# A fourth pair of weight chunks by seven products in the last two blocks, and mixed weights made by GpSimd in the first and second

## The reference

```python
xn = layernorm(x)
s = silu(xn @ w_gate.T)                       # 2752 gate units
_, idx = top_k(-abs(s), 1376)                 # the smaller half of each token's gates by magnitude ...
s = s.at[rows, idx].set(0.0)                  # ... is set to 0
a = (s * (xn @ w_up.T)) @ w_down.T
h = relu(xn @ up_w) ** 2                      # 2048 shared units
moe = ((xn @ fc1_w) @ expert_w) * sum(top_k(xn @ gate_w, 2)[0])
f = layernorm(h @ down_w + moe @ fc2_w, gamma, beta)
y = x + a + f
```

## The kernel before

| m | step |
|---|---|
| 0-7 | the last, narrow gate chunk (5), with the router's logits |
| 8-91 | three pairs of chunks by seven products each, 28 granules a pair: gate 0 and 1, gate 2 and 3, gate 4 and up 4 |
| 92-123 | latent, hidden 0 and 1, routed 0 and 1 |
| 124-171 | shared 0 and 1, hidden 2 and 3, shared 2 and 3 |
| 172-203 | up chunks 0 to 3, 8 granules each |
| 204-247 | out 0 and 1, 22 granules each |

## Time and profile before

### The profile page before, as it was taken

How to read it: one execution, slowest core, us unless ns; L and a number is a source line. 1 busy time by engine, 2 the same in 40 slices (tenths; PEclk the granted TensorE clock), 3 DMA queues, 4 the chain that set the end, 5 groups by cost and what they waited for, 6 DMA issues and landing times.

```text
span 2333.7 us, 27748 instructions
## 1 busy us (share of the span) xinstructions
PE 2317.7 (99%) x10504; PEld 1927.2 (83%) x10504; DVE 1634.8 (70%) x1810; ACT 1086.9 (47%) x1253; POOL 829.3 (36%) x682
## 2 busy tenths in 40 slices
PE   8999999999999999999999999999999999999999
PEld 6888888888877888888888888888888888888887
DVE  4349999976265989897334598898723568989850
ACT  3247776223233787722124387761213448785110
POOL 5467878796444021123024321304004413030500
PEclk9999999999999999999999999999999999999999
DMA  7798878878898666665778766665667865556555
GB/s 277 280 394 294 292 245 311 293 243 310 287 363 302 206 196 191 204 201 180 234 237 277 249 194 193 195 209 189 207 219 255 279 221 195 193 192 214 180 190 180
DMA packets 191047, 558.43 MB, mean 239 GB/s; under 512 B 20161, under 2 KB 29377, under 8 KB 190913
## 3 DMA queue, kind: packets, MB, share of 16 engines
q1 hardware_dynamic: 190912, 556.65, 71.0%
HBM read 429.62 MB, written 126.94 MB: 238 GB/s over the span
## 4 chain that ended last, share of the span: by engine, by line
PE 93%; DMA 3%; DVE 1%; SPq 1%; POOL 1%; ACT 0%; issue 0%; DVEq 0%; ACTq 0%
PE bank L945 30%; PE bank L947 30%; PE bank L946 30%; PE bank L965 2%; DMA mixed_w<-mixes 1%; DMA split_w<-w 1%; DMA w<-mixed_w 1%; PE bank L956 1%; POOL w L732 0%; SPq L565 0%; SPq L569 0%; PE bank L1038 0%; PE bank L1039 0%; DMA raw<-w_gate_dram 0%; POOL w L735 0%
## 5 line engine op out<-in xcount | busy, mean ns | idle before, releaser
L1292 DVE TENSOR_SCALAR_CACHE_REDUCE junk_v<-mag,cand 128x2816 bf16<-128x2816 f32 x248 | 780.3, 3146 | 8.8
L786 ACT ACTIVATE junk_s<-mag,cand 128x2816 uint8<-128x2816 f32 x248 | 655.4, 2643 | 222.2 <-DVE cand L1284 195.7
L945 PE MATMUL bank<-w,tok 128*128 128x512 f32 (+1 forms) x952 | 365.8, 384 | 1.8 <-DMA w<-split_w 1.7
L947 PE MATMUL bank<-w,tok 128*128 128x512 f32 (+1 forms) x952 | 364.3, 383 | 0.0
L946 PE MATMUL bank<-w,tok 128*128 128x512 f32 (+1 forms) x952 | 364.1, 382 | 0.0
L732 POOL TENSOR_TENSOR w<-raw,w 128x512 fp32r<-128x512 f32 (+1 forms) x196 | 268.1, 1372 | 77.5 <-ACT w L774 67.8
L945 PE MATMUL bank<-w,prod_t 128*128 128x512 f32 x672 | 269.4, 401 | 0.0
L947 PE MATMUL bank<-w,prod_t 128*128 128x512 f32 x672 | 262.8, 391 | 0.0
L946 PE MATMUL bank<-w,prod_t 128*128 128x512 f32 x672 | 261.9, 390 | 0.0
L945 PE MATMUL bank<-tok,w 128*128 128x512 f32 x640 | 249.0, 389 | 0.0
L946 PE MATMUL bank<-tok,w 128*128 128x512 f32 x640 | 249.0, 389 | 0.0
(11 more groups left out here) (149 smaller groups left out, 3728.3 us busy)
## 6 DMA issues: line engine op xcount, KB each, us to landing
...
split_w<-w SPq DMA_DIRECT2D x192, 512.0 KB, 4.9
...
w<-mixed_w SPq DMA_DIRECT2D x108, 256.0 KB, 3.5
...
```

What stands on the lines that cost most here:

```text
L786: act.activation(junk_s[:, :, :], mag[:, :, t, :], ACT.Sign, scale=-1.0, bias=cand[:, t:t + 1], accum_out=cnt[:, t:t + 1]).then_inc(counte ...
L945: pe.matmul(out, left[0], right[0], start=first, stop=False)
L947: return pe.matmul(out, left[1], right[0], start=False, stop=last)
L1292: dve.tensor_scalar(junk_v[:, :, :], mag[:, :, t, :], cand[:, t:t + 1], float(1 - (GATED - KEPT)), ALU.is_lt, ALU.add, accum_out=cnt[:, t: ...
```

## The change

In blocks 2 and 3 a fourth pair, up chunks 0 and 1, is made by seven products behind the third, and the plain steps of these two chunks are left out (`FAST`). These blocks have 260 granules: pairs 8 to 119, latent from 120, shared 2 and 3 to 199, up 2 and 3 from 200 to 215, `out` from 216. The first turn stands behind granule 211, and bank 0 holds up chunk 2 there as before.

- `prod` can't hold `S3` and `S4` and the results of this pair, so in blocks 2 and 3 these sums lie in `acc` and are split at granules 10 and 12, once the last block's outputs are stored (`sums_acc`).
- The hidden units need the rows of up 0 and 1, so SP writes these results, 1 MB a chunk, to DRAM behind the pair (`spill`, at granule 123) and loads them back behind shared 3 (`load_back`, at 199). VectorE gives each its sign (`sign_up`, now with `g`) right ahead of its mask.
- Two steps of the search stand beside the fourth pair (granules 101 and 108), the other 29 at 122 to 199, every 2.75 granules; `drop_ties` at 202, masks from 203 on. Shared chunk 3 is read at 203.
- The third pair's mixes are made in block 0 and the fourth's in block 1, one set of four operations per k-step, by GpSimd (`late_mix`) at `at + 11`, in `raw_more` or `raw`. SP loads a set's four pieces at `at` to `at + 6` and stores four at `at + 14`, with `at` = 36, 54, 72, 90 in block 0 and 96, 114, 132, 150 in block 1. `mix_later` and what belonged to it are gone.

```diff
...
-PAIRS = [(("gate", 0), ("gate", 1)), (("gate", 2), ("gate", 3)), (("gate", GC - 2), ("up", GC - 2))]
-FAST = len(PAIRS)
+PAIRS = [(("gate", 0), ("gate", 1)), (("gate", 2), ("gate", 3)), (("gate", GC - 2), ("up", GC - 2)),
+         (("up", 0), ("up", 1))]
+FAST = [0, 3, 4, 4]
 FIRST_PAIRS = 2
+UP_PAIR, SPILLED_PAIR = 2, 3
 PRODUCTS = ["A11 B11", "S2 T2", "A12 B21", "S1 T1", "S4 B22", "S3 T3", "A22 T4"]
-PRODUCT_BANK = [[4, 6, 0, 2, 4, 6, 0], [2, 4, 6, 4, 6, 0, 2], [4, 6, 0, 4, 6, 0, 2]]
+PRODUCT_BANK = [[4, 6, 0, 2, 4, 6, 0], [2, 4, 6, 4, 6, 0, 2], [4, 6, 0, 4, 6, 0, 2],
+                [4, 6, 0, 4, 6, 0, 2]]
...
-        steps = _middle + _last
+        steps = [step for step in _middle + _last if step[0] not in sum(PAIRS[:FAST[b]], ())]
...
+            self.signs_at = {end["fast", p, q] + FAST_LAG + 3: (p, q) for p in range(UP_PAIR) for q in (5, 6)}
+            up_end = end["fast", UP_PAIR, 6]
+            self.signs_at[last + 4 if up_end == last else up_end + FAST_LAG + 3] = (UP_PAIR, 6)
+        if later and FAST[b] > SPILLED_PAIR:
+            first = up_end + FAST_LAG + 4
+            steps_at = [first, first + 7]
+            steps_at += [last + 3 + (11 * k + 3) // 4 for k in range(BITS + 1 - len(steps_at))]
         else:
-            self.search_from = end[("gate", GC - 2)] + LAG + 1
-        self.search_at = {self.search_from + 3 * k: k for k in range(BITS)}
-        self.search_end = self.search_from + 3 * BITS
+            first = last + 5 if later else end[("gate", GC - 2)] + LAG + 1
+            steps_at = [first + 3 * k for k in range(BITS + 1)]
+        self.search_at = {m: k for k, m in enumerate(steps_at[:BITS])}
+        self.search_from, self.search_end = first, steps_at[BITS]
...
-        self.mask_at = {max(self.search_end + 1 + i, end.get(("up", g), 0) + LAG + 1): g
+        self.back_at = end[("shared", 3)] if FAST[b] > SPILLED_PAIR else None
+        read = {("up", c): self.back_at + 5 + 2 * c for c in range(2)} if self.back_at else {}
+        read.update({key: end[key] + LAG for key in end})
+        self.mask_at = {max(self.search_end + 1 + i, read.get(("up", g), 0) + 1): g
                         for i, g in enumerate(GROUPS[:-1])}
...
-MIX_BLOCK = 1
-MIX_LOADS = {8: range(8, 10), 32: range(10, 11), 40: range(11, 12)}
-MIX_AT = {24: 8, 32: 9, 44: 10, 52: 11}
-MIX_STORES = {26: 8, 34: 9, 46: 10, 54: 11}
+LATE_SETS = {FIRST_MIXES + n: (0, 36 + 18 * n) for n in range(HALF)}
+LATE_SETS.update({FIRST_MIXES + HALF + n: (1, 96 + 18 * n) for n in range(HALF)})
+LATE_LOADS = [{at + 2 * i: (n, i) for n, (b, at) in LATE_SETS.items() for i in range(4) if b == c} for c in range(BLOCKS)]
+LATE_AT = [{at + 11: n for n, (b, at) in LATE_SETS.items() if b == c} for c in range(BLOCKS)]
+LATE_STORES = [{at + 14: n for n, (b, at) in LATE_SETS.items() if b == c} for c in range(BLOCKS)]
...
-SUMS_HI_AT = {2: 4, 4: 3}
-SUMS_LO_AT = {2: 4, 4: 3}
+SUMS_HI_AT = [{}, {2: 4, 4: 3}, {10: 4, 12: 3}, {10: 4, 12: 3}]
+SUMS_LO_AT = [{}, {2: 4, 4: 3}, {10: 4, 12: 3}, {10: 4, 12: 3}]
...
+        sums_acc = {i: [over(f"sums{i}_acc{part}", [P, HALF, 2 * P], F32R, acc_at + 8 * N * (2 * (i - 3) + part))
+                        for part in range(2)] for i in (3, 4)}
+        assert 32 * N == TILES * HID * 4
+        def sums_of(b, i):
+            return sums_acc[i] if i > 2 and FAST[b] > SPILLED_PAIR else sums[i]
...
-            def load_mix(n):
+            def load_late_mix(n, i):
                 p, k = n // HALF, n % HALF
-                if n < FIRST_MIXES + 2:
-                    sp.wait_ge(stored, 16 * (MIX_BLOCK * 2 * TILES + 1))
+                if n == FIRST_MIXES:
+                    sp.wait_ge(mixes_made, 4 * FIRST_MIXES)
                 else:
-                    sp.wait_ge(mixes_stored[n % 2], 16 * (n // 2))
-                for i in range(4):
-                    src, width = words_of((PAIRS[p][i // 2], k + i % 2 * HALF))
-                    sp.dma_start(mix_place(n, i), src).then_inc(mix_loaded[n % 2], 16)
-            def store_later_mix(n):
-                sp.wait_ge(later_mixes, 4 * (n - FIRST_MIXES) + 4)
-                words = acc[:, 2 * (n % 2):2 * (n % 2) + 2, :].rearrange("p t (i n) -> p t i n", n=N)
-                sp.dma_start(mixed_w[n].rearrange("(t i) p n -> p t i n", i=2), words).then_inc(mixes_stored[n % 2], 16)
+                    sp.wait_ge(late_stored, 64 * (n - FIRST_MIXES))
+                if n in LATE_AT[1].values():
+                    sp.wait_ge(lo_ready, FIRST_PLAN.count)
+                src, width = words_of((PAIRS[p][i // 2], k + i % 2 * HALF))
+                sp.dma_start(late_place(n, i), src).then_inc(late_loaded, 16)
+            def store_late_mix(n, i):
+                sp.wait_ge(late_mixes, 4 * (n - FIRST_MIXES) + 4)
+                sp.dma_start(mixed_w[n, i], late_place(n, i)).then_inc(late_stored, 16)
+            def spill(b, c):
+                for q in (4, 5) if c else (2, 6):
+                    for j in range(2):
+                        bank, value = emptied(b, ("fast", SPILLED_PAIR, q, j))
+                        sp.wait_ge(bank_emptied[bank], value)
+                sp.dma_start(spilled_u[c], prod[:, 4 * c:4 * c + 4, :, :]).then_inc(spilled[c], 16)
+            def load_back(b, c):
+                sp.wait_ge(spilled[c], 16 * spills(b))
+                sp.dma_start(prod[:, 4 * c:4 * c + 4, :, :], spilled_u[c]).then_inc(up_back[c], 16)
...
+                if m in LATE_LOADS[b]:
+                    load_late_mix(*LATE_LOADS[b][m])
+                if m in LATE_STORES[b]:
+                    for i in range(4):
+                        store_late_mix(LATE_STORES[b][m], i)
+                if plan.back_at:
+                    if m == plan.fast_end + 4:
+                        spill(b, 1)
+                        spill(b, 0)
+                    if m == plan.back_at:
+                        load_back(b, 0)
+                        load_back(b, 1)
...
+            def late_mix(n):
+                b11, b21, b12, b22 = (late_place(n, i) for i in range(4))
+                at = 4 * (n - FIRST_MIXES)
+                pool.wait_ge(late_loaded, 64 * (n - FIRST_MIXES + 1))
+                pool.tensor_tensor(b11, b12, b11, ALU.subtract).then_inc(late_mixes, 1)
+                pool.tensor_tensor(b12, b22, b12, ALU.subtract).then_inc(late_mixes, 1)
+                pool.wait_ge(late_mixes, at + 1)
+                pool.tensor_tensor(b22, b22, b11, ALU.subtract).then_inc(late_mixes, 1)
+                pool.wait_ge(late_mixes, at + 3)
+                pool.tensor_tensor(b21, b21, b22, ALU.subtract).then_inc(late_mixes, 1)
...
+                if i > 2 and FAST[b] > SPILLED_PAIR:
+                    act.wait_ge(stored, 16 * (b * 2 * TILES + 1))
+                elif i > 2:
                     act.wait_ge(bank_filled, filled(b - 1, ("out", 1, TILES - 1)))
...
+            def sign_up(b, g):
+                ks = slice(4 * g, 4 * g + 4)
+                dve.wait_ge(signs_done, b * (GC + 1) + PLANS[b].signs_before[g] + 1)
+                if g < 2:
+                    dve.wait_ge(up_back[g], 16 * spills(b))
+                else:
+                    for j in range(2):
+                        for q in (4, 5):
+                            bank, value = emptied(b, ("fast", UP_PAIR, q, j))
+                            dve.wait_ge(bank_emptied[bank], value)
                 dve.scalar_tensor_tensor(out=prod[:, ks, :, :], in0=positive[:, ks, :, :], scalar=-1.0,
                                          in1=prod[:, ks, :, :], op0=ALU.add, op1=ALU.mult).then_inc(up_signed, 1)
...
+                if (b, g) in SIGNED and g < 2:
+                    sign_up(b, g)
                 ks = slice(4 * g, min(4 * g + 4, GK))
                 for t in range(TILES):
-                    if b and g == GC - 2:
-                        dve.wait_ge(up_signed, b)
+                    if (b, g) in SIGNED:
+                        dve.wait_ge(up_signed, SIGNED.index((b, g)) + 1)
...
```

119 lines of the change are left out of this document (54 added, 65 removed).

## The result

The changed kernel takes **2353.7 us** (median of four runs, 2352.2 to 2355.1) against 2334.7 us before, timed beside it: the ratio is 1.008, with a 95% interval from 1.0064 to 1.0096. It is slower by 19 us. The forecast was 2352 us, with "slower" at 0.80.

A forecast was written before the change was run, and what follows sets the result against it. TensorE, busy 99% of the span, was taken to bound the kernel. From the profiled 2335.8 us: -10.9 - 5.3 + 0.5 + 1.8 + 30.4 - 0.4 gave 2352 us, range 2331 to 2362 us.

The forecast's parts named there:

- Part 1: Blocks 2 and 3: seven products for eight on up chunks 0 and 1, 5.4 us less per block, -10.9 us.
- Part 2: Block 1: the third pair's mixes leave it, so its slow stretch should look like block 2's, -5.3 us.
- Part 3: Block 0: the third pair's mixes added on GpSimd, with their loads and stores, +0.5 us, ends 0 and 3.
- the sentence that the sum doesn't change by the shared read port: Block 0: GpSimd's added work sharing VectorE's SBUF read port doesn't change the sum; nothing was added for it.
- the loads behind granules 36 to 42: Block 0's tight place: each mix load issued there can push a raw load back by some tenths of a us.
- Part 4: Start of blocks 2 and 3: sums split at granules 10 and 12 delay a low half, +0.9 us per block, +1.8 us.
- Part 5: Blocks 2 and 3: the search makes VectorE late, TensorE stands 15.2 us at each first turn, +30.4 us.
- the 13 to 17 us: Sign of being right: one TensorE gap this long ahead of the first turn in blocks 2 and 3.
- the case of 9 to 20 us: Main case: TensorE's stall at the first turn is this long per block in blocks 2 and 3; chance 0.72.
- the term for VectorE's own waits: Blocks 2 and 3: VectorE waiting for ScalarE's counts and TensorE's banks, 18.6 us before, 11 kept, ends 0 and 18.6.
- The laying hit the row of before: Check on the waits: operations laid end to end put the earlier kernel's threshold at 1583.0; the row says 1583.07.
- a `thr` more than 33 us ahead of the turn: Blocks 2 and 3: sign of being wrong, meaning ScalarE's waits fell; some 29 us was expected.

The follow-up runs named there:

- Experiment 7: Changed kernel with up chunk 2 read earlier, mask 2 later and sums earlier in blocks 2 and 3, and block 0's search spread over 103 granules: 2331.4 us.
- experiment 3: Changed kernel without the fourth pair in any block, sums at their old places, third pair's mixes still on GpSimd in block 0: 2337.6 us.
- Experiments 4 and 6: Changed kernel: 4 with GpSimd's block 0 mixes on 8 of 512 columns, 2344.0 us; 6 with block 0's search over 103 granules for 93, 2354.4 us.
- experiment 1: Changed kernel with VectorE's read of up chunk 2 moved ahead of up chunk 0's sign and mask in blocks 2 and 3: 2339.6 us.

## Why the prediction came out right

The time was right to 2 us and the mechanism that decides held. But the terms of blocks 2 and 3 were 5 us too high and that of block 0 was 6 us too low.

- **Part 1 (-10.9): right.** In the changed kernel it can't be seen apart from the stall. Experiment 7 shows blocks 2 and 3 at 563.2 and 563.1 us for 568.3 and 568.1, -10.1 with the sums' share in it. The extra loads cost nothing.
- **Part 2 (-5.3): right.** Block 1 is 568.2 us, and 568.4 in experiment 3. That the fourth pair's mixes are free in block 1 holds as well. The cause fits too. Between 640 and 720 us the DMA engines were 98.9% busy before and 87.4% after, and the loads of mixed weights landed sooner (the last number is the median in us, before and then after; the window begins 16 us into block 1 before and 11 us after). Whether VectorE's part of the mixes had a share is not shown, since it moved too.

```profile
w<-mixed_w SPq DMA_DIRECT2D x29, 256.0 KB, 7.1
```

```profile
w<-mixed_w SPq DMA_DIRECT2D x30, 256.0 KB, 3.7
```

- **Part 3 (+0.5, ends 0 and 3): wrong, it is +6.4.** The step that failed is the sentence that the sum doesn't change by the shared read port, since most of VectorE's time in block 0 is the count over one input and "its turn point there has slack of its own". The place that the forecast did name, the loads behind granules 36 to 42, cost 0.9 us here and between nothing and 0.7 us in the experiments; the other 5.5 us are the wait for the hidden subtraction and the slow matmuls behind it. The count was indeed untouched (3.15 us in every row), and the hidden subtractions and `settle` were not. The group of the hidden subtractions between 200 and 385 us, before and then after (columns: times | busy us, mean ns | idle before):

```profile
L1434 DVE TENSOR_TENSOR hidden<-squares,hidden 128x512 fp32r<-128x512 f32 x16 | 16.5, 1054 | 0.0
```

```profile
L1503 DVE TENSOR_TENSOR hidden<-squares,hidden 128x512 fp32r<-128x512 f32 x16 | 18.8, 1202 | 0.0
```

  These 2.3 us are half of the 4.8 us by which the last of them is late; 0.6 us came from `settle`, and VectorE was 1.6 us late at 200 us already. That would be harmless with room, and there was none: VectorE was busy for 180.5 of these 185 us, and TensorE was already waiting for the last hidden subtraction. I looked for slack at GpSimd and at the turn, and did not look at VectorE's hidden subtractions in between. Experiments 4 and 6 show both halves of it: without GpSimd's work, or with more room on VectorE, this wait goes. The rule that I cited from the Trainium skill ("Perfetto Trace Analysis", Optimizing Scalar/DVE Operations) would have been the better guide here.
- **Part 4 (+1.8): the size about right, the cause only in part.** The waits are 2.3 us in block 2 and 0.5 in block 3; by the blocks' lengths they cost 2.5 and 0.9, together 3.4. Only the 0.9 us for GpSimd's low half in block 2, and 0.3 in block 3, are of the kind that was forecast. The larger part waits for VectorE's read of a product, and it was 0.2 us in experiment 1.
- **Part 5 (+30.4): the mechanism right, the size too large.** There is one gap in each of blocks 2 and 3, at the first turn, released by VectorE's read of up chunk 2, of 9.3 us for 15.2. That is below the 13 to 17 us that I had named as the sign of being right, and just inside the case of 9 to 20 us that had a chance of 0.72. The step behind it is the term for VectorE's own waits. I kept 11 us, and this is what the search of block 2 shows:

```profile
DVE refused L1350 <- ACT junk_s L861: 4.9, 4, 2.2
```

The first count of the third step began at 1370.88, 1.2 us after the latent product (forecast 1.3), and `thr` was written at 1584.78, 215.1 us after that product began; by the forecast's terms it would be 221.4. That is the whole miss of 6. "The laying hit the row of before" was weak evidence: it agreed in the total, with a ScalarE count taken as 2.83 us where the page's mean is 2.64 us. From `thr` to the read the forecast was 43.3 us and the trace has 43.7 (1584.78 to 1628.45), so the masks, the signs and GpSimd's share were sized well together. The first sign operation took 3.37 us: it stood at 1611.62 behind a product of GpSimd that ran until 1612.85, and the next product took 3.34 us in place of 1.5. The second sign met no product under way and took its 2.28 us. So a sign waited for at most one product and held up the next, as the prediction had reckoned.

What the forecast lacked is the tail of a stall: 2.1 and 2.8 us of half-rate matmuls behind them. So a stall of 9.3 us costs 11.4 to 12.1. Together Parts 1, 4 and 5 were forecast at +21.3 and measured +16.3 (8.7 and 7.6), and block 0 stood at +0.5 for +6.4. The total hit to 2 us because 5 us too much and 6 us too little cancel, and that part of the agreement is luck. I had named a `thr` more than 33 us ahead of the turn as a sign against me, and it came 35 us ahead: it rightly told that ScalarE's waits had fallen.
